# An attention block on one core: two key tiles for each column-tiled visit of TensorE, row maxima of two heads at once with the mask added on VectorE, fp32r masks, and the division by the row sums moved to the output stage

## The chip, the core and the metric

One core of one Trainium2 chip runs the whole program. The metric is the device time of one execution in microseconds. Engines: PE is TensorE (PEld its weight loads), DVE VectorE, ACT ScalarE, POOL GpSimd, SP SyncE, which here only issues DMAs.

## The reference, cut to what matters

Two batches of 2048 rows of 1024 channels, 32 query heads of 32 channels, 8 key and value heads, causal attention, and a gate with a low-rank routed part:

```python
xn = _layernorm(x, axis=-1)
q = (xn @ wq).reshape(b, s, 32, 32); k, v = 8 heads each, repeated 4 times
scores = jnp.where(causal, jnp.einsum('bihd,bjhd->bhij', q, k) * SCALE, finfo.min)
attn = jax.nn.softmax(scores, axis=-1)
s = jnp.einsum('bhij,bjhd->bihd', attn, v).reshape(b, s, 1024) @ wo
g = _silu(xn @ W_base.T + b_base + routed_low_rank(xn))
out = x + s * g
```

## The kernel before

Four functions follow each other, each a block that ends with all engines done: `project` (layer norm, q, k, v, written to scratch in HBM), `attend`, `gate` and `output`. High and low parts (`_hi`, `_lo`) carry fp32 products in fp32r matmuls.

`attend` works on 16 groups (batch and key head), each with 4 query heads (`NREP`). The queries of a group are cut into 4 chunks of 512 (`CPB`, `CH`); chunk c sees 4(c+1) key tiles of 128, so a group has 16, 32, 48 and 64 score tiles, 160 in all. `stage(c)` writes out the order of the operations of chunk c, and every engine walks that one list:

- "T", j, h (L796 to L809): scores of key tile j against the 512 queries of head h, keys on the partitions, into one of two PSUM banks `cols_ps` (`NCOLS`). On the diagonal a second matmul adds the mask (L807, bf16), and the width shrinks to 384, 256, 128. ACT takes the exponential into `probs[j % 4]` (L887). T number h+2 may start only when the exponential of number h is done.
- "S" (L743): scores with the queries on the partitions, only for the row maximum. It runs 72 pieces (`LEAD`) ahead, in one of four banks `rows_ps`; a piece on the diagonal has a mask matmul too (L750, bf16). DVE reduces each piece to a maximum (L905). The maxima of a chunk are turned ("M", L753, L915) and sent by a DMA to the last row of `q_st[c]`, so that T subtracts them.
- "V", j (L810): the weighted values of key tile j, four matmuls for four heads side by side on 32 columns of the array each (`tile_position`), and the same again for the second pass of fp32. "L", j (L826): the row sums of tile j with a matrix of ones, in the same form, but only for the tiles that POOL doesn't add up (`ADDS`); "Y" (L835): the row sums of what POOL has added. V for tile j stands at step j + 2 after the second T, L for it after the fourth. I call one such stay in the column form a visit. V and L of a tile are two visits.
- "O" (ACT copies `o_ps` and `l_ps`), "I" (eight reciprocals of 64 columns on DVE, L949), "N" (DVE multiplies, L956, and SP stores the normalised chunk).

SP walks the same list: it loads the q chunks for the next group, the row of maxima, and stores. In `gate` and `output` TensorE works on one tile of 128 rows after the other, three matmuls for each product, two PSUM banks. In `output` SP's order for tile n is: store half 0, store half 1 (both wait for DVE), then load the attention result, x and g of tile n + 2 (`load`, L1126). ACT rounds to `t_hi`, DVE subtracts to `t_lo`, and DVE's list for tile n is `finish(n)`, then `low(n + 2)`.

Of the kernel before, what the change touches and what calls it, by code (L numbers as in the profile page):

```python
# [483 lines left out]
def pieces_of(c):  # L484

    return [(i, h, p, min(CH, (TPC * c + i + 1) * P - CH * p))
            for i in range(TPC) for h in range(NREP) for p in range(c + 1)]

PIECES = [(c, n == len(pieces_of(c)) - 1, piece) for c in range(CPB) for n, piece in enumerate(pieces_of(c))]
NPG = len(PIECES)
# [3 lines left out]
assert NPG == NTG  # L496
LEAD = 72
TURN_AFTER = 2
NROWS, NCOLS = 4, 2
NSLICE = 8  # L500


def piece_at(i):

    return (i // NPG, *PIECES[i % NPG])


def stage(c):

    steps, old = TPC * (c + 1), TPC * ((c - 1) % CPB + 1)
    order = []
    for j in range(steps):
        for h in range(NREP):
            t = T_OFF[c] + NREP * j + h  # L520
            order.append(("T", j, h))
            order.append(("S", *piece_at(t + LEAD)))
            turned = piece_at(t + LEAD - TURN_AFTER)
            if turned[2]:
                order.append(("M", turned[0], turned[1]))
            if j == 0 and h == 1:
                order += [("V", old - 2, "before"), ("L", old - 2, "before")]
            if j == 0 and h == 3:
                order += [("V", old - 1, "before"), ("L", old - 1, "before"), ("Y", "before")]
            if j == 1 and h == 1:  # L530
                order.append(("O",))

            slot = (NREP * (j - 2) + h) // (1 if c == 0 else 2)
            if 0 <= slot < NSLICE and (c == 0 or h % 2):
                order.append(("I", slot))
            if j >= 2 and h == 1:
                order.append(("V", j - 2))
            if j >= 2 and h == 3:
                order.append(("L", j - 2))
        if j == (3 if c == 0 else 5):  # L540
            order.append(("N",))
    return order
# [5 lines left out]
def before(op):  # L548
    return op[0] in ("O", "I", "N") or op[-1] == "before"


def first_uses():

    out = []
    for i in range(LEAD):
        out.append(("S", *piece_at(i)))
        if i >= TURN_AFTER and piece_at(i - TURN_AFTER)[2]:
            out.append(("M", *piece_at(i - TURN_AFTER)[:2]))
# [4 lines left out]
USES = [sum(op[0] in "SM" for op in st) for st in STAGES]  # L563
NSG = sum(USES)
S_OFF = [len(FIRST_USES) + sum(USES[:c]) for c in range(CPB)]
assert NSG % NROWS == 0


ADDS = {"pool": [[], [0, 1, 3, 4, 6], [0, 1, 3, 4, 6, 7, 9, 10], [0, 1, 3, 4, 6, 7, 9, 10, 12, 13]]}


def adds_through(who, c, j):

    return sum(max(0, len(a) - 1) for a in ADDS[who][:c]) + sum(1 for t in ADDS[who][c][1:] if t <= j)


def adds_of_group(who):
    return adds_through(who, CPB - 1, NJG)


def attend(nc, sc, ident, ident_b, mask_ij, mask_ji, wb, lb, gw_hi, gw_lo):

    ctx = ExitStack()
    with ctx:
# [11 lines left out]
        probs = [sb(f"probs{i}", [P, NREP, CH]) for i in range(4)]  # L596
        added = {who: sb(f"added_{who}", [P, NREP, CH]) for who in ADDS}
        neg_max = [sb(f"neg_max{i}", [P, NREP * TPC, CPB]) for i in range(2)]
        shift = sb("shift", [P, 16], FP32R)
        row = [sb(f"row{i}", [16, P]) for i in range(2)]  # L600
        o_raw = [sb(f"a_o_raw{i}", [P, CH]) for i in range(2)]
        l_raw = [sb(f"l_raw{i}", [P, CH]) for i in range(2)]
        o_sb = [sb(f"o_sb{i}", [P, CH]) for i in range(2)]
        gw_raw = sb("gw_raw", [P, 4, D])
# [669 lines left out]
```

## Time and profile before

| | us |
|---|---|
| median of 3 runs (3853.81 to 3854.62) | 3854.03 |
| span of the profiled execution | 3855.3 |
| PE busy in it | 3712.1 (96%) |
| PEld, DVE busy | 2272.1 (59%), 2212.6 (57%) |
| ACT, POOL busy | 1557.0 (40%), 1379.6 (36%) |

The page gives no other time of the profiled execution than its span; it is 1.3 us over the median. `project` runs to about 670 us, the first exponential of `attend` stands at 703.96 and the last matmul at about 3078, `gate` runs to about 3494, `output` to the end. In the listed rows a busy time counts the overlap of pipelined matmuls once, and a duration is from issue to end, so start-to-start distances tell TensorE's pace, not durations.

### The profile page before, as it was taken

How to read it: one execution, taken by the hardware profiler on the slowest of the kernel's cores; microseconds unless marked ns; L12 is line 12 of the kernel's file. 1: busy time of each engine (PE TensorE's matmuls, PEld its weight loads, DVE VectorE, ACT ScalarE, POOL GpSimd, SP SyncE). 2: the span in 40 equal slices, each digit the busy share in tenths (PEclk: the TensorE clock that was granted, in tenths of full speed). 3: DMA queues.
4: the chain of work that ended last, by engine and by line, in shares of the span. 5: the costliest groups of instructions: out<-in, count | busy, mean ns of one | idle time of the engine just before them, and what ended most of it. 6: DMA issues, size and time to landing. Idle time of an engine off the chain costs nothing. (4 is left out here: it accounts for less than half of the span.)

```text
span 3855.3 us, 66009 instructions
## 1 busy us (share of the span) xinstructions
PE 3712.1 (96%) x21376; PEld 2272.1 (59%) x21376; DVE 2212.6 (57%) x4099; ACT 1557.0 (40%) x3042; POOL 1379.6 (36%) x349
## 2 busy tenths in 40 slices
PE   7999998999999999999999999999999889998999
PEld 6888886544444444444444444444444378887887
DVE  5343332877777777777777677777777322222333
ACT  3122210455555555555555555555555511011000
POOL 0000000465565574565465565555655600000000
PEclk9999998799999999999999999999999999999999
DMA  6555444211101102101101111111010054444555
GB/s 219 167 175 159 153 145 146 79 34 35 46 20 49 38 23 48 39 26 45 43 26 45 37 32 42 35 35 45 21 47 18 6 179 145 137 137 162 191 189 174
DMA packets 232906, 326.87 MB, mean 85 GB/s; under 512 B 16800, under 2 KB 132512, under 8 KB 231072
## 3 DMA queue, kind: packets, MB, share of 16 engines
q1 hardware_dynamic: 229008, 310.48, 26.7%
q10 hardware_dynamic: 3600, 12.58, 1.0%
q8 instruction: 167, 2.74, 0.3%
q14 instruction: 131, 1.07, 0.1%
HBM read 188.25 MB, written 134.22 MB: 84 GB/s over the span
## 5 line engine op out<-in xcount | busy, mean ns | idle before, releaser
L905 DVE TENSOR_REDUCE neg_max<-rows_ps 128x1 f32<-128x512 f32 (+3 forms) x2560 | 1434.3, 602 | 600.7 <-PE rows_ps L747 427.2
L887 ACT ACTIVATE probs<-cols_ps 128x512 f32<-128x512 f32 (+3 forms) x2560 | 1270.4, 533 | 1059.4 <-PE cols_ps L804 542.9
L737 POOL TENSOR_TENSOR added_pool<-added_pool,probs 128x2048 f32<-128x2048 f32 (+2 forms) x272 | 1137.0, 4180 | 296.6 <-ACT probs L887 285.5
L804 PE MATMUL cols_ps<-q_st,k_st 97*128 97x512 f32 (+3 forms) x2560 | 1089.6, 428 | 61.7 <-ACT probs L887 42.9
L747 PE MATMUL rows_ps<-k_st,q_st 96*128 96x512 f32 (+3 forms) x2560 | 1021.7, 405 | 16.9 <-DMA q_st<-scratch_q_hi 16.9
L804 PEld LDWEIGHTS cols_ps<-q_st,k_st 97*128 97x128 f32 x2560 | 488.2, 191 | 820.6 <-ACT probs L887 702.8
L821 PE MATMUL o_ps<-probs,v_st 128*32 128x512 f32 (+3 forms) x5120 | 605.7, 545 | 0.0
L747 PEld LDWEIGHTS rows_ps<-k_st,q_st 96*128 96x128 f32 x2560 | 510.6, 200 | 40.9 <-issue 17.1
L737 POOL TENSOR_TENSOR added_pool<-probs 128x2048 f32<-128x2048 f32 x48 | 219.5, 4573 | 726.3 <-ACT probs L887 726.3
L949 DVE RECIPROCAL l_raw<-l_raw 128x64 f32<-128x64 f32 x512 | 275.3, 540 | 56.2 <-ACT a_o_raw L897 56.2
L438 PE MATMUL acc<-xt_hi,w_hi 128*128 128x512 f32 x704 | 281.6, 400 | 0.6 <-DVE logits L381 0.6
L440 PE MATMUL acc<-xt_hi,w_lo 128*128 128x512 f32 x704 | 277.6, 394 | 0.0
L439 PE MATMUL acc<-xt_lo,w_hi 128*128 128x512 f32 x704 | 276.8, 393 | 0.0
L720 POOL TENSOR_TENSOR gw_lo<-gw_raw,gw_hi 128x1024 fp32r<-128x1024 f32 x9 | 21.0, 2372 | 672.3 <-ACT gw_hi L862 672.3
L750 PE MATMUL rows_ps<-mask_ij,ident_b 128*128 128x128 bf16 x1024 | 241.8, 236 | 0.0
L395 DVE SCALAR_TENSOR_TENSOR out_lo<-acc,out_hi 128x512 fp32r<-128x512 f32 x80 | 55.3, 692 | 324.4 <-ACT out_hi L290 324.4
L1082 PE MATMUL g_acc<-gw_hi,g_t_hi 128*128 128x512 f32 x576 | 225.2, 391 | 16.9 <-DMA g_t_lo<-scratch_hw_lo 16.9
L807 PE MATMUL cols_ps<-mask_ji,ident_b 128*128 128x128 bf16 x1024 | 237.9, 232 | 0.0
L831 PE MATMUL l_ps<-probs,ones 128*32 128x512 f32 (+3 forms) x2176 | 228.0, 491 | 0.0
L1083 PE MATMUL g_acc<-gw_lo,g_t_hi 128*128 128x512 f32 x576 | 224.9, 390 | 0.0
L1084 PE MATMUL g_acc<-gw_hi,g_t_lo 128*128 128x512 f32 x576 | 224.8, 390 | 0.0
L1202 PE MATMUL o_acc<-ow_hi,o_t_hi 128*128 128x512 f32 x512 | 200.4, 391 | 11.2 <-DVE o_t_lo L1168 11.2
(101 smaller groups left out, 3155.0 us busy)
## 6 DMA issues: line engine op xcount, KB each, us to landing
q_st<-scratch_q_hi SPq DMA_DIRECT2D x128, 256.0 KB, 4.4
x_sb<-in_x SPq DMA_DIRECT2D x32, 512.0 KB, 4.0
scratch_xt_hi<-xt_hi SPq DMA_DIRECT2D x32, 512.0 KB, 6.0
scratch_xt_lo<-xt_lo SPq DMA_DIRECT2D x32, 512.0 KB, 6.8
scratch_q_hi<-out_hi SPq DMA_DIRECT2D x64, 256.0 KB, 2.4
scratch_q_lo<-out_lo SPq DMA_DIRECT2D x64, 256.0 KB, 2.9
q_st<-scratch_q_lo SPq DMA_DIRECT2D x64, 256.0 KB, 4.6
scratch_o<-o_sb SPq DMA_DIRECT2D x64, 256.0 KB, 2.4
```

The source lines that it names most:

```text
L438: nc.tensor.matmul(out, lh, rh, start=(k == 0), stop=False)
L439: nc.tensor.matmul(out, lh, rl, start=False, stop=False)
L440: ins = nc.tensor.matmul(out, ll, rh, start=False, stop=(k == KT - 1))
L737: nc.gpsimd.tensor_tensor(added["pool"][:, :, q0:CH], a[:, :, q0:CH], probs[j % 4][:, :, q0:CH], ALU.add).then_inc(pool_added, 1)
L747: ins = nc.tensor.matmul(out[:, 0:keys], q_st[c][0:K1, h, i * P:(i + 1) * P], k_st[kbuf][0:K1, CH * p:CH * p + keys], start=True, stop=p < c)
L750: ins = nc.tensor.matmul(out[:, keys - P:keys], ident_b[:, :], mask_ij[:, :], start=False, stop=True)
L804: ins = nc.tensor.matmul(cols_ps[h % NCOLS][:, q0:CH], k_st[u][:, j * P:(j + 1) * P], q_st[c][:, h, q0:CH], start=True, stop=not diagonal)
L807: ins = nc.tensor.matmul(cols_ps[h % NCOLS][:, q0:q0 + P], ident_b[:, :], mask_ji[:, :], start=False, stop=True)
L821: ins = nc.tensor.matmul(o_ps[h * HD:(h + 1) * HD, q0:CH], v_st[vbuf][:, j, :], probs[j % 4][:, h, q0:CH], start=(j == 0), stop=(j == step ...
L887: nc.scalar.activation(probs[j % 4][:, h, q0:CH], cols_ps[h % NCOLS][:, q0:CH], ACT.Exp) \
L905: nc.vector.tensor_reduce(neg_max[chunk % 2][:, r, p:p + 1], rows_ps[bank % NROWS][:, 0:keys], AX.X, ALU.max, negate=True).then_inc(rows_f ...
L949: ins = nc.vector.reciprocal(l_raw[cp % 2][:, part], l_raw[cp % 2][:, part])
```

## The change

- S: the list is now made of units, two heads of one block of 128 queries and one chunk of keys. Both heads' matmuls go into one slot of two banks (`rows_ps` is 2 slots of 2 banks), and one semaphore count covers both. Below the diagonal DVE reduces both at once; on it there is no mask matmul, DVE runs a tensor_tensor_reduce for each head, which adds `tri` (fp32 in SBUF), writes the sum in bf16 and keeps the maximum. `LEAD` is 40 units, that is 80 pieces.
- T: its mask and the identity are fp32r, no longer bf16.
- V, L and Y become "W": at every even step j it takes the values of tiles j - 4 and j - 3, then the row sums of those of the two that POOL doesn't add, then, at the end of a chunk, those that POOL has added. `probs` has 5 buffers, not 4. POOL's lists are shorter (18 additions for a group, were 20), each addition is cut in two halves of two heads, and it alternates between two sums.
- ACT copies `o_ps` and `l_ps` to buffers that SP stores as they are. The reciprocals and the product leave `attend`. `gate` loads all row sums, inverts them in 8 parts of 128 columns on DVE, and ACT's queue stores them.
- `output` loads for each tile, beside the attention result, the inverted sums with four DMAs (each repeats the 8 rows of a head on 32 partitions), DVE multiplies (`norm`), and SP's and DVE's orders change as shown.
- The loads of `gw_raw` at the start of `attend` have 2 buffers, not 4.

```diff
 def stage(c):
             t = T_OFF[c] + NREP * j + h
             order.append(("T", j, h))
-            order.append(("S", *piece_at(t + LEAD)))
+            ahead, chunk, last, unit = unit_at(t // 2 + LEAD)
+            order.append(("S", ahead, h % 2, chunk, last, unit))
...
+            if j % 2 == 0 and h == 1:
+                order.append(("W", old - 4 + j, "before") if j < 4 else ("W", j - 4))
+            if j == 2 and h == 1:
+                order.append(("K",))
+            if j == 2 and h == 3:
                 order.append(("O",))
...
-ADDS = {"pool": [[], [0, 1, 3, 4, 6], [0, 1, 3, 4, 6, 7, 9, 10], [0, 1, 3, 4, 6, 7, 9, 10, 12, 13]]}
+ADDS = [[], [0, 1, 3, 4, 6], [0, 1, 3, 4, 6, 8, 10], [0, 1, 3, 4, 6, 8, 9, 11, 13]]
...
+            def row_scores(use, slot, kbuf, half, c, i, p, hp):
+                if half == 0:
+                    pe.wait_ge(rows_free, use + 1)
+                keys = keys_of(c, i, p)
+                ins = nc.tensor.matmul(rows_ps[slot][:, half, 0:keys], q_st[c][0:K1, 2 * hp + half, i * P:(i + 1) * P],
+                                       k_st[kbuf][0:K1, CH * p:CH * p + keys], start=True, stop=True)
+                if half == 1:
+                    ins.then_inc(rows_full, 1)
...
+            def unit_max(full, slot, c, i, p, hp):
+                wait_apart(dve, rows_full, full, passed_rows)
+                if p < c:
+                    nc.vector.tensor_reduce(row_max[c % 2][:, 2 * hp:2 * hp + 2, i, p], rows_ps[slot][:, :, :], AX.X, ALU.max) \
+                        .then_inc(rows_free, 1)
+                    return
+                keys = keys_of(c, i, p)
+                for half in range(2):
+                    ins = nc.vector.tensor_tensor_reduce(masked_rows[slot][:, half, 0:keys], rows_ps[slot][:, half, 0:keys],
+                                                         tri[:, CH - keys:CH], 1.0, MASKED, ALU.add, ALU.max,
+                                                         row_max[c % 2][:, 2 * hp + half, i, p:p + 1])
+                ins.then_inc(rows_free, 1)
...
+            def weigh(n, u, c, op):
+                pe.wait_ge(probs_ready, n.lin(NTG, T_OFF[cc] + NREP * (j0 + 2) + NCOLS - back * NTG))
+                for j in (j0, j0 + 1):
+                    ...
+                        ins = nc.tensor.matmul(o_ps[h * HD:(h + 1) * HD, q0:CH], v_st[vbuf][:, j, :],
+                                               probs_of(cc, j)[:, h, q0:CH], start=(j == 0), stop=(j == steps - 1),
+                                               tile_position=(0, h * HD))
...
@@ output, SP
                 for u in range(2):
                     n = Step(pair, u)
+                    if not last:
+                        wait_apart(sp, t_lo_ready, n.lin(1, 1), passed)
+                        load_o(n.lin(1, 2), b, u)
                     for half in range(2):
                         wait_apart(sp, y_ready, n.lin(2, half + 1), passed)
...
                     if not last:
-                        load(n.lin(1, 2), b, u)
+                        load_xg(n.lin(1, 2), u)
@@ output, DVE
+            def norm(n, u):
+                dve.wait_ge(t_loaded[u], n.pair * 80 + 80)
+                nc.vector.tensor_mul(o_raw[u][:, :, :], o_raw[u][:, :, :], l_inv[u][:, :, :]).then_inc(norm_ready, 1)
...
+            norm(Step(0, 0), 0)
+            norm(Step(0, 1), 1)
             low(Step(0, 0), 0)
             low(Step(0, 1), 1)
             with dve.Fori(0, NPAIR - 1) as pair:
                 for u in range(2):
+                    norm(Step(pair + 1, u), u)
                     finish(Step(pair, u), u)
                     low(Step(pair + 1, u), u)
```

## Rows read from the trace of the kernel before

**Rows 1.** Windows of one group and of output: us, then busy by engine

```profile
1746.06:1893.10 147.04, 143.99 (x934) 69.45 (x932) 109.81 (x205) 82.60 (x169) 84.77 (x20) 1.00 0.15 37
3550.00:3855.00 305.00, 301.26 (x1330) 249.12 (x1328) 108.14 (x139) 28.64 (x27) 0.00 (x0) 1.00 0.55 187
```

**Rows 2.** Timeline of PE, one step below the diagonal: start, us, line

```profile
1844.24 0.50 PE L804 MATMUL cols_ps<-q_st,k_st 97*128 97x512 f32 x1
...
1844.82 0.40 PE L804 MATMUL cols_ps<-q_st,k_st 97*128 97x512 f32 x1
...
1845.43 0.50 PE L804 MATMUL cols_ps<-q_st,k_st 97*128 97x512 f32 x1
...
1846.00 0.41 PE L804 MATMUL cols_ps<-q_st,k_st 97*128 97x512 f32 x1
...
1846.48 1.07 PE L821 MATMUL o_ps<-probs,v_st 128*32 128x512 f32 x8
1847.48 0.50 PE L804 MATMUL cols_ps<-q_st,k_st 97*128 97x512 f32 x1
```

**Rows 3.** Timeline of weight loads in that step, with the idle time before

```profile
1845.43 0.19 PEld L804 LDWEIGHTS cols_ps<-q_st,k_st 97*128 97x128 f32 x1 [0.22 <-ACT probs L887]
```

**Rows 4.** Timeline of ACT in that step

```profile
1844.78 1.09 ACT L887 ACTIVATE probs<-cols_ps 128x512 f32<-128x512 f32 x2 [0.93 <-PE cols_ps L804]
1846.05 1.09 ACT L887 ACTIVATE probs<-cols_ps 128x512 f32<-128x512 f32 x2 [0.18 <-PE cols_ps L804]
```

**Rows 5.** Timeline of PE on the diagonal

```profile
1889.24 0.28 PE L804 MATMUL cols_ps<-q_st,k_st 97*128 97x256 f32 x1
...
1889.73 0.22 PE L804 MATMUL cols_ps<-q_st,k_st 97*128 97x128 f32 x1
...
1890.68 0.85 PE L821 MATMUL o_ps<-probs,v_st 128*32 128x384 f32 x8
1891.47 0.33 PE L804 MATMUL cols_ps<-q_st,k_st 97*128 97x128 f32 x1
```

**Rows 6.** Groups by form, 725 to 3130 us: busy, mean ns, idle

```profile
L905 DVE TENSOR_REDUCE neg_max<-rows_ps 128x1 f32<-128x512 f32 x1738 | 1128.6, 681 | 471.5 <-PE rows_ps L747 420.6 <-PE rows_ps L750 34.8 <-issue 5.4
...
L807 PEld LDWEIGHTS cols_ps<-mask_ji,ident_b 128*128 128x128 bf16 x1008 | 98.0, 97 | 105.8 <-issue 70.0
```

**Rows 7.** DVE's product of two SBUF tiles: ns min/median/max

```profile
L956 DVE TENSOR_TENSOR o_sb<-a_o_raw,l_raw x64: 691/1369/2641, 745.4 to 3082.6; 128x512 f32<-128x512 f32 x64
```

**Rows 8.** Timelines around the start and the end of attend

```profile
L720 POOL TENSOR_TENSOR gw_lo<-gw_raw,gw_hi x9: 2352/2377/2382, 675.8 to 694.4; 128x1024 fp32r<-128x1024 f32 x9
...
3079.17 3.43 DVE L949 RECIPROCAL l_raw<-l_raw 128x64 f32<-128x64 f32 x8 [45.62 <-ACT a_o_raw L897]
```

**Rows 9.** Timeline of SP's queue in output, one tile

```profile
3712.10 0.41 SPq L1127 DMA_DIRECT2D o_raw<-scratch_o  x1
...
3713.35 0.38 SPq L1129 DMA_DIRECT2D o_g<-scratch_g  x1
```

**Rows 10.** Timeline of DVE in output, one tile

```profile
3709.86 0.69 DVE L1177 SCALAR_TENSOR_TENSOR o_prod<-o_acc,o_g 128x512 f32<-128x512 f32 x1 [0.69 <-PE o_acc L1204]
3710.59 0.69 DVE L1181 TENSOR_TENSOR o_y<-o_prod,o_x 128x512 f32<-128x512 f32 x1
3717.36 1.23 DVE L1168 TENSOR_TENSOR o_t_lo<-o_raw,o_t_hi 128x1024 fp32r<-128x1024 f32 x1 [6.08 <-ACT o_t_hi L1155]
3718.50 0.68 DVE L1177 SCALAR_TENSOR_TENSOR o_prod<-o_acc,o_g 128x512 f32<-128x512 f32 x1
...
3720.74 0.69 DVE L1177 SCALAR_TENSOR_TENSOR o_prod<-o_acc,o_g 128x512 f32<-128x512 f32 x1 [0.83 <-PE o_acc L1204]
```

**Rows 11.** DMA issues by line: KB each, median us to landing

```profile
v_st<-scratch_v SPq DMA_DIRECT2D x16, 256.0 KB, 7.5
...
out<-o_y SPq DMA_DIRECT2D x28, 256.0 KB, 2.0
```

**Rows 12.** Windows of 1 us in output; last columns DMA share, GB/s

```profile
3717.00:3718.00 1.00, 1.00 (x6) 0.84 (x5) 0.64 (x1) 0.33 (x1) 0.00 (x0) 1.00 0.99 406
```

More of the change, by code:

```diff
@@ L555, in first_uses, with adds_through, attend @@
     for i in range(LEAD):
-        out.append(("S", *piece_at(i)))
-        if i >= TURN_AFTER and piece_at(i - TURN_AFTER)[2]:
-            out.append(("M", *piece_at(i - TURN_AFTER)[:2]))
+        for half in range(2):
+            ahead, chunk, last, unit = unit_at(i)
+            out.append(("S", ahead, half, chunk, last, unit))
+        if i >= TURN_AFTER and unit_at(i - TURN_AFTER)[2]:
+            out.append(("M", *unit_at(i - TURN_AFTER)[:2]))
     return out
 FIRST_USES = first_uses()
-USES = [sum(op[0] in "SM" for op in st) for st in STAGES]
+NFIRST = sum(map(ends_use, FIRST_USES))
+USES = [sum(map(ends_use, st)) for st in STAGES]
 NSG = sum(USES)
-S_OFF = [len(FIRST_USES) + sum(USES[:c]) for c in range(CPB)]
-assert NSG % NROWS == 0
-ADDS = {"pool": [[], [0, 1, 3, 4, 6], [0, 1, 3, 4, 6, 7, 9, 10], [0, 1, 3, 4, 6, 7, 9, 10, 12, 13]]}
[L572 to L581, printed above, removed]
+S_OFF = [NFIRST + sum(USES[:c]) for c in range(CPB)]
+assert NSG % NSLOT == 0
+ADDS = [[], [0, 1, 3, 4, 6], [0, 1, 3, 4, 6, 8, 10], [0, 1, 3, 4, 6, 8, 9, 11, 13]]
+NADD = sum(len(a) - 1 for a in ADDS if a)
+def adds_through(c, j):
+    return 2 * (sum(max(0, len(a) - 1) for a in ADDS[:c]) + sum(1 for t in ADDS[c][1:] if t <= j))
+def attend(nc, sc, ident, ident_r, mask_ji, tri, wb, lb, gw_hi, gw_lo):
     ctx = ExitStack()
@@ L775, in run @@
                     kind = op[0]
-                    if kind in "VLY":
-                        old = op[-1] == "before"
-                        cc = (c - 1) % CPB if old else c
-                        back = 1 if old and c == 0 else 0
-                        steps = TPC * (cc + 1)
-                        to_sum = [j for j in range(steps) if not any(j in ADDS[who][cc] for who in ADDS)]
-                        adders = [who for who in ADDS if ADDS[who][cc]]
                     if kind == "S":
-                        ahead, chunk, _, piece = op[1:]
-                        if piece == pieces_of(chunk)[0]:
+                        ahead, half, chunk, _, unit = op[1:]
+                        if half == 0 and unit == units_of(chunk)[0]:
                             pe.wait_ge(q_loaded[chunk], n.lin(48, 48 * (1 + ahead)))
@@ L845, in _ @@
+                    elif kind == "W":
+                        weigh(n, u, c, op)
+                    use += ends_use(op)
             over_stages(pe, run)
@@ L887, in run @@
-                        nc.scalar.activation(probs[j % 4][:, h, q0:CH], cols_ps[h % NCOLS][:, q0:CH], ACT.Exp) \
+                            g = J_OFF[c] + j - NPROBS
+                            act.wait_ge(values_done, n.lin(NVG, g // 2 + 1 + 3))
+                            back = 1 if g < 0 else 0
+                            c5 = CPB - 1 if back else max(cc for cc in range(CPB) if J_OFF[cc] <= g)
+                            j5 = g + back * NJG - J_OFF[c5]
+                            first_group = isinstance(n.pair, int) and n.pair == 0 and u == 0
@@ L1139, in pair_of_tiles @@
                     if not last:
-                        load(n.lin(1, 2), b, u)
-            load(0, 0, 0)
-            load(1, 0, 1)
+                        load_xg(n.lin(1, 2), u)
+            for u in range(2):
+                load_o(u, 0, u)
+                load_xg(u, u)
             with sp.Fori(0, NPAIR // 2 - 1) as pair:
```

403 lines of the change are left out of this document (201 added, 202 removed).

## The prediction

> **What bounds the kernel now.** I read the windows first. In one whole group of attend (147.04 us, one of 16) TensorE is busy for 143.99 us, DVE for 109.81, ACT for 82.60, POOL for 84.77; in output TensorE is busy for 301.26 of 305 us [rows 1]. So TensorE looks like the bound in both, at full granted clock (1.00, the 2.4 GHz level). But a busy TensorE isn't one at its peak, so the timeline of one step comes second [rows 2]. The reader is to see three distances there, from one T to the next. Just after a visit a pair T, S takes 0.58 us (1844.24 to 1844.82). The third T comes 0.61 us after the second, and its weight load had idled for ACT [rows 3]. From the visit's start to the next T it is 1.00 us (1846.48 to 1847.48). ACT's own timeline tells why the third T waits [rows 4]: the exponential of the first begins at 1844.78, 0.04 us after the T ends (1844.24 + 0.50), takes 0.60, and the T that needs its bank starts 0.05 later, at 1845.43. With two banks that is a loop: two Ts take 0.50 + 0.04 + 0.60 + 0.05 = 1.19 us, however fast TensorE is. After the first head of a tile, where ACT also waits for other engines, the lag is 0.12 instead of 0.04 (1845.93 to 1846.05), and the loop 1.27. So below the diagonal attend is bound by this loop between visits and by TensorE in visits. ACT stands idle in a visit (0.93 us before 1844.78) and can't catch up later, for only two scores lie ready.
>
> **The change part by part.** All sums are against the span, 3855.3 us; the median of the runs is 1.3 lower, and so is my number.
>
> *Price of a pass.* A visit on 512 columns takes 1.00 us, one on 384 columns 0.79 [rows 2, 5]; 128 columns cost 0.21, so 512 cost 0.86 and the switch itself 0.14. The T after it has its weight load exposed, and so has a T that waited for ACT: 0.10 more, for a pair takes 0.58 there, and 0.49 on the diagonal where the weights were loaded in time (1889.24 to 1889.73 [rows 5], T of 256 columns, mask, S of 512). That row also gives the price of a mask: six steps of 128 columns at 0.06 are 0.36, so 0.13 is left for it.
>
> *Merged visits.* By the code a group has 51 visits now (40 V, 11 separate L) and 20 after. If TensorE were the bound, 31 x 0.24 x 16 = 119 us would go. I go through eight Ts between two visits below the diagonal instead. Starts: 0, 0.58, 1.19 (loop), 1.77 (its weights exposed again), 2.45 (loop 1.27), 3.02, 3.64, 4.21; then S and into the visit, 4.78, less 0.06 since three S pieces in ten are narrower, and 0.14 for the switch: 4.86 us besides the passes. Twelve such stretches in a group: 58.3. On the diagonal TensorE sets the pace, with 0.61, 0.55, 0.49, 0.43 for T, mask, S at 512 to 128 columns of T (0.49 is the row): the stretch over widths 512, 384, 256 comes to 4.7, that over 256, 128 and the next chunk's 512 to 4.0. Four of each: 34.8. Passes after, in full widths: V 34, L 14.25, Y 3, so 51.25 x 0.86 = 44.1; before it was 49.5, so the shorter lists of POOL cost 1.5 us a group. ACT's two copies hold the loop up by 0.8 us a chunk, 3.2, as now; the turned shift 0.4 a chunk, 1.6. Sum 142.0, against 147.04.
>
> *Row maxima.* The S masks (1024 of them) vanish from TensorE; in the stretches above they are already left out. On DVE one reduction of 1024 columns stands for two of 512 at 0.68 each [rows 6]: between 0.68 and 1.36, and I take 1.22, near the upper end, since the elements are as many. The two slots free up in larger lumps: unit 3 must wait for the reduction of unit 1. Below the diagonal that comes just in time (unit 1 complete at 1.21, reduced at 2.47, unit 3's first S at 2.79). On the narrow tiles units come every 1.0 us, and I count 0.25 us a chunk for DVE: 1.0 a group. The masked reduction has no row. Its nearest are the plain one (0.68) and the product of two SBUF tiles, 0.69 at least, median 1.37 beside POOL's additions [rows 7]; I take 0.7, since only one of its inputs is in SBUF. The group is then 143.0: 4.0 less, and over 15 full groups -60 us.
> The Trainium skill says the same of it: "SBUF — State Buffer", section "SBUF: two separate sides", has GpSimd and VectorE lock each other out only for a two-port mode or two SBUF inputs. By that the 1.37 doesn't apply; the slow case is a rival below, since no run here shows it.
>
> *fp32r masks in T.* A bf16 identity loads in 0.10 us, an fp32r weight in 0.19 [rows 3, 6]. Either the load hides under the T (and a change of type between two loads vanishes), or it shows on narrow Ts. 1024 x (-0.07 to +0.09) = -70 to +95 us; I take 0, because the T before it is 512 columns wide or has an exposed load in most places.
> The skill's "TensorE: Matmul & The Clock Gate", section "Weight-path perf modes — Fast Weight Load (FWL) and DoubleRow", allows the fast load only for types that aren't fp32. It speaks against this edit: the row agrees for the load (0.10 against 0.19), and the whole price would be the +95 end.
>
> *Start and end of attend.* With two buffers the nine pieces of the gate's weights (POOL 2.38 us each, the last from 694.4 [rows 8]) end later than the first S units do: 0 to +12, taken +4, with the longer lead. At the end the reciprocals (3.43 us [rows 8]) and the product go, but two more tiles of values stand after the last exponential: -3. In gate the reciprocals (8 x about 1 us) lie under the matmuls of a half tile, which take at least the 5.4 us of one in output (half of 10.88 [rows 10]); nothing, and 1 us each if that cover were gone.
>
> *Output.* Here a loop through the DMAs becomes long. SP issues the loads of tile n + 2 after the stores of tile n - 1 and the loads of x and g for n + 1, and DVE must multiply tile n + 2 before it finishes tile n; TensorE waits for that finish to get its bank for n + 1. Count from Y, the end of DVE's work on tile n - 1 (3710.59 + 0.69 = 3711.28 [rows 10]). The first load is issued at Y + 0.82, the next ones 0.6 apart [rows 9]; seven now, so the last at Y + 4.6. The engines then move x, g, the result and the sums, 2 MB, at 406 GB/s at best with a DMA share of 0.99 [rows 12], and about 300 for packets of 512 B; flow starts 1.9 after the issue, so the sums have landed at Y + 2.7 + 2.7 + 1.7 + 1.7 = Y + 8.8. From there norm 1.15 (1.23 long, next start 1.14 later [rows 10]), then four steps of 0.72: the next Y is at 8.8 + 4.0 = 12.8. A tile now takes 10.88 (3709.86 to 3720.74 [rows 10]). So TensorE idles 2.0 us a tile, 29 tiles: +58. At the start norm of both tiles stands ahead of the first low part, behind all fourteen DMAs: +6. Together +64. Bounds: if the last DMA needed only 2.0 us from its issue, it lands at 6.6 and no time is lost; if it needed 7.5, as the loads of values do [rows 11], a tile takes 16.1 and it is +157.
>
> Sum: 3855.3 - 60 + 0 + 1 + 64 = 3860, as a median 3859.
>
> **The rivals.**
> 1. *The sums land in time.* The loss in output begins only when they land later than about Y + 7.6 (norm 1.15 and prod 0.69 must end before tile n + 1 starts at Y + 9.4). If the queue drains 1.2 us sooner than I count, output keeps its pace: 3859 - 58 = 3801. For it: the four DMAs are only 128 KB each, and DMA share is 0.55 on average [rows 1]. Against it: seven issues in a row, and DVE's order.
> 2. *TensorE, not the exponential's loop, is the bound of attend.* Then the visits give 119, the S masks 1024 x 0.13 = 133, less 24 for passes: -228 instead of -60, 3691. Against it is the idle weight load [rows 3], 0.22 us before each third T.
> The skill's "TensorEngine Tiling (Array Packing)", section "Key Properties", has TensorE drained by each change of tiling mode. The row agrees with 0.14 us; by that rule alone each visit saved would count, which is this rival.
> 3. *Slower: the masked maxima wait for POOL.* If tensor_tensor_reduce with `tri` in SBUF takes 1.37 instead of 0.69 [rows 7], a masked unit takes 2.7 us against 1.2 between units, and the S two units later waits; 32 units x 16 x about 0.5 = +250, 4109. It decides once a masked unit takes over about 1.8 us.
> 4. *Slower: the sums land late*, at 7.5 us from the issue: 3859 + 99 = 3958.
>
> **How the numbers follow.** My forecast (output waits, the loop eats most of attend's gain) gets 0.45, with its own range 3815 to 3905 from DVE's lumps and the masks; rival 1 0.30, rival 2 0.10, rival 3 0.07, rival 4 0.08. The range for 8 in 10 leaves out rivals 2 and 3 and the ends of the others: 3765 to 3960. A measurement here can tell about 0.2%, 8 us, from no change. Forecast: faster 0.15, same 0.08, slower 0.22. Rival 1: 0.26, 0.02, 0.02. Rival 2: faster 0.09, same 0.01. Rivals 3 and 4: slower 0.15. Sum: faster 0.50, same 0.11, slower 0.39.
>
> **What would show it.** In output the distance from tile to tile (12.8 against 10.88), TensorE's idle time before a tile with DVE's prod as releaser, and norm's start released by a DMA. In attend a group of about 143 us, the third T still released by the exponential, visits of 0.14 + 0.86 for each pass. The masked reduction at 0.7 us and a 1024-column one at 1.2. The T, mask, S of 128 and 256 columns stays at 0.43 and 0.49, or is up to 0.09 slower if the fp32r load shows. I am wrong if output keeps its pace, if a group is under 140 us, or if DVE holds up TensorE below the diagonal.

## The result

The changed kernel takes 4198.8 us (median of 4 runs, 4185.1 to 4205.8) against 3854.3 us for the kernel before on the same chip: ratio 1.0887, 95% interval 1.0872 to 1.0902. It is 8.9% slower, where 3859 us were forecast, and outside the range. Its span is 4194.2 us, 338.9 more than 3855.3. Read from the two traces by first and last instruction of each stage:

| stretch | before, us | after, us | difference | forecast |
|---|---|---|---|---|
| up to the first exponential | 704.0 | 715.4 | +11.4 | +4 |
| attend, first to last exponential | 2372.0 | 2459.4 | +87.4 | -60 |
| its end and gate | 413.0 | 410.1 | -2.9 | -3 |
| gate's last matmul to output's first | 11.3 | 32.1 | +20.8 | +6 |
| output, 32 tiles | 351.0 | 573.2 | +222.2 | +58 |

The windows of the kernel after that answer to [rows 1]: the same odd group of attend, the even group ahead of it, and output. The columns are as there: us, busy PE, PEld, DVE, ACT, POOL, then PEclk, DMA share, GB/s.

```profile
1797.68:1948.33 150.65, 142.44 (x886) 74.07 (x886) 88.43 (x185) 83.26 (x168) 79.22 (x36) 0.98 0.14 36
1638.14:1797.68 159.54, 146.35 (x885) 75.18 (x884) 88.10 (x185) 83.12 (x168) 79.17 (x36) 0.95 0.14 35
3620.00:4190.00 570.00, 415.63 (x1530) 328.28 (x1529) 152.45 (x186) 31.72 (x30) 0.00 (x0) 0.86 0.56 139
```

TensorE now idles 8 to 13 us in a group, where before it idled 3 in an odd one; in output it idles for 154 us, and its granted clock is 0.86 there on average. Two things are to be explained: the output stage, and an attend that has less work on TensorE (142.4 us busy against 144.0) and takes longer.

**Output.** First DVE's timeline of one tile in the kernel after (it answers to [rows 10]; the bracket is the idle time before), then SP's queue that feeds it ([rows 9]), then the chain that ended last, in order of time.

```profile
4000.97 0.69 DVE L1206 TENSOR_TENSOR o_y<-o_prod,o_x 128x512 f32<-128x512 f32 x1
...
4016.23 1.23 DVE L1189 TENSOR_TENSOR o_raw<-o_raw,o_l_inv 128x1024 f32<-128x1024 f32 x1 [13.43 <-DMA o_l_inv<-scratch_l_inv]
4017.37 0.68 DVE L1202 SCALAR_TENSOR_TENSOR o_prod<-o_acc,o_g 128x512 f32<-128x512 f32 x1
```

```profile
4000.58 1.70 SPq L1157 DMA_DIRECT2D out<-o_y  x2
4002.46 0.35 SPq L1145 DMA_DIRECT2D o_x<-in_x  x1
4002.91 0.40 SPq L1146 DMA_DIRECT2D o_g<-scratch_g  x1
4003.59 0.38 SPq L1139 DMA_DIRECT2D o_raw<-scratch_o  x1
4004.16 3.63 SPq L1141 DMA_DIRECT2D o_l_inv<-scratch_l_inv  x4
```

```profile
3893.76 9.63 DMA o_l_inv<-scratch_l_inv
...
3912.08 9.81 DMA o_l_inv<-scratch_l_inv
...
3930.31 10.12 DMA o_l_inv<-scratch_l_inv
```

The loop is the one the prediction described: seven issues, a landing, norm, and only then the end of tile n that frees TensorE's bank. Its period is 18.4 us instead of 12.8. DVE waits 13.4 us for the row sums before it can do 4 us of work. The chain shows the last of the four DMAs on its way for 8.5 to 11.2 us in each tile, about 9.8 at the median. Windows of 1 us while only these DMAs are under way:

```profile
4012.00:4013.00 1.00, 0.34 (x2) 0.00 (x0) 0.00 (x0) 0.00 (x0) 0.00 (x0) 1.00 0.75 47
4014.00:4015.00 1.00, 0.00 (x0) 0.00 (x0) 0.00 (x0) 0.00 (x0) 0.00 (x0) 1.00 0.76 70
```

The DMA engines are three quarters busy and move 47 to 70 GB/s, where I had put 300.

**Attend.** A stretch in the middle of an odd group, windows of 1 us, and TensorE's timeline at its end:

```profile
1825.00:1826.00 1.00, 0.51 (x3) 0.25 (x2) 1.00 (x4) 1.00 (x3) 0.99 (x1) 1.00 0.00 0
1826.00:1827.00 1.00, 0.58 (x3) 0.39 (x3) 0.28 (x4) 0.91 (x3) 0.00 (x0) 1.00 0.05 20
1827.00:1828.00 1.00, 0.87 (x4) 0.57 (x5) 0.29 (x1) 1.00 (x2) 0.00 (x0) 1.00 0.66 250
...
1830.00:1831.00 1.00, 1.00 (x8) 0.22 (x4) 0.41 (x1) 0.00 (x0) 1.00 (x2) 0.50 0.00 0
1831.00:1832.00 1.00, 1.00 (x8) 0.00 (x0) 0.00 (x0) 0.00 (x0) 1.00 (x1) 0.50 0.00 0
```

```profile
1826.42 0.49 PE L839 MATMUL cols_ps<-q_st,k_st 97*128 97x512 f32 x1 [0.91 <-ACT probs L889]
...
1828.96 3.53 PE L798 MATMUL o_ps<-probs,v_st 128*32 128x512 f32 x16
1832.42 0.54 PE L839 MATMUL cols_ps<-q_st,k_st 97*128 97x512 f32 x1
```

TensorE waited (busy 0.51 and 0.58 of two windows, here while ACT copied O and L out), and then its granted clock is 0.50, the 1.2 GHz level, and a visit of two tiles takes 3.46 us from its start to the next T; at full clock the same x16 takes 1.85. For a part of it ACT has nothing to do (0.00 of two windows). Over attend the kernel before has 50.6 us at the low level, the kernel after 205.8. 6 of these spells begin in attend before, 38 after; one more is under way as attend starts, and its rest, 13 and 18 us, is in the sums. At half speed the difference is at most (205.8 - 50.6) / 2 = 78 of the 87 us.

Not each wait brings the clock down. From 900 to 3000 us the kernel after has 120 windows of 1 us, not at the low level, in which TensorE is busy for less than 0.6, and 32 falls; each fall stands no more than 2.2 us behind such a stretch, but most of the stretches have no fall behind them.

### The profile page after: what moved, and what is told of

The parts are those of the page before. It is cut to its first block and busy times, and to the rows that moved or that the text cites. A ratio compares the mean times of both kernels' runs of the same rounds, so it can differ in the third digit from the quotient of the medians.

```text
span 4194.2 us, 64097 instructions
## 1 busy us (share of the span) xinstructions
PE 3775.0 (90%) x20608; PEld 2392.3 (57%) x20608; DVE 1906.4 (45%) x3821; ACT 1564.8 (37%) x3042; POOL 1290.6 (31%) x603
## 5 line engine op out<-in xcount | busy, mean ns | idle before, releaser
L906 DVE TENSOR_REDUCE row_max<-rows_ps 128x2 f32<-128x1024 f32 x768 | 933.1, 1225 | 725.1 <-PE rows_ps L755 715.8
L738 POOL TENSOR_TENSOR added<-added,probs 128x1024 f32<-128x1024 f32 (+2 forms) x480 | 1040.6, 2193 | 481.4 <-ACT probs L889 481.4
L911 DVE CUSTOM_DVE_ANT_0 masked_rows<-rows_ps,tri 128x128 bf16<-128x128 f32 (+3 forms) x1024 | 458.6, 487 | 304.5 <-PE rows_ps L755 290.2
L738 POOL TENSOR_TENSOR added<-probs 128x1024 f32<-128x1024 f32 x96 | 226.3, 2379 | 717.6 <-ACT probs L889 717.6
L1230 PE MATMUL o_acc<-ow_hi,o_t_hi 128*128 128x512 f32 x512 | 230.5, 450 | 186.5 <-DVE o_prod L1202 154.4
L798 PEld LDWEIGHTS o_ps<-probs,v_st 128*32 128x32 f32 x5120 | 140.2, 114 | 290.9 <-issue 221.7
L842 PE MATMUL cols_ps<-mask_ji,ident_r 128*128 128x128 f32 x1024 | 245.6, 240 | 0.0
L1230 PEld LDWEIGHTS o_acc<-ow_hi,o_t_hi 128*128 128x128 f32 x512 | 111.7, 218 | 224.0 <-DVE o_prod L1202 167.0
L1176 ACT ACTIVATE o_t_hi<-o_raw 128x1024 fp32r<-128x1024 f32 x32 | 33.8, 1057 | 546.8 <-DVE o_raw L1189 533.4
L1189 DVE TENSOR_TENSOR o_raw<-o_raw,o_l_inv 128x1024 f32<-128x1024 f32 x32 | 39.2, 1225 | 426.1 <-DMA o_l_inv<-scratch_l_inv 426.1
```

Of the source, the lines that this page charges most:

```text
L738: nc.gpsimd.tensor_tensor(into[:, heads, q0:CH], other[:, heads, q0:CH], probs_of(c, j)[:, heads, q0:CH], ALU.add).then_inc(pool_added, 1)
L798: ins = nc.tensor.matmul(o_ps[h * HD:(h + 1) * HD, q0:CH], v_st[vbuf][:, j, :], probs_of(cc, j)[:, h, q0:CH], start=(j == 0), stop=(j == s ...
L842: ins = nc.tensor.matmul(cols_ps[h % NCOLS][:, q0:q0 + P], ident_r[:, :], mask_ji[:, :], start=False, stop=True)
L906: nc.vector.tensor_reduce(row_max[c % 2][:, 2 * hp:2 * hp + 2, i, p], rows_ps[slot][:, :, :], AX.X, ALU.max) \
L911: ins = nc.vector.tensor_tensor_reduce(masked_rows[slot][:, half, 0:keys], rows_ps[slot][:, half, 0:keys], tri[:, CH - keys:CH], 1.0, MASK ...
L1230: nc.tensor.matmul(acc[half][:, :], t_hi[u][:, k, :], w_hi[:, k, cols], start=(k == 0), stop=False)
```

## The experiments

Each was timed beside the kernel before on the same chip; that kernel's median was 3853.1 to 3856.6 us in the three rounds, so a difference between times of two rounds carries some 3 us. "Low" is the time in attend at the 1.2 GHz level, counted as above. What a tile of output takes is the median distance from tile to tile.

### Output: the division taken out

```diff
-                for h in range(NREP):
-                    sp.dma_start(l_inv[u][h * HD:(h + 1) * HD, :, :], sc["l_inv"]...partition_broadcast(HD))
-                nc.vector.tensor_mul(o_raw[u], o_raw[u], l_inv[u]).then_inc(norm_ready, 1)
+                dve.sem_inc(norm_ready, 1)
```

> The changed kernel without the division in output: the four loads of inverted sums for each tile and the multiplication are left out, so the attention result isn't divided. Everything else of the change stays, SP's new order too. Theory (the sums' loads and the order on VectorE make all of output's loss): a tile takes 10.9 us again, output loses about 220 us and its start 10, so 3965 to 3975, and what is left over the kernel before, 110 to 120 us, belongs to attend and its start. Rival (SP's new order costs by itself): above 12 us a tile, over 4000.

3964.2 us, ratio 1.0270 (1.0248 to 1.0293). Output is back at its old pace (352.6 us against 351.0), so the division costs 4198.8 - 3964.2 = 235 us, and everything else in the change 110. The way from gate's last matmul to output's first is 14.9 us, against 32.1 with the division and 11.3 before. Attend is nearly unchanged (2464.9 us, low 218.1 in 44 spells): the two losses are separate.

### Output: DVE's order

```diff
-                    norm(Step(pair + 1, u), u)
                     finish(Step(pair, u), u)
+                    norm(Step(pair + 1, u), u)
                     low(Step(pair + 1, u), u)
```

> The changed kernel with one line moved: in output VectorE finishes tile n before it multiplies tile n + 2. Theory (the order on VectorE puts the landing of the sums on the path of every tile): with the order mended a tile takes as long as the DMA engines need for its 2.5 MB, which in the changed kernel is about 14 us (6 for x, g, the result and the stores, 8 for the sums at 60 GB/s), or the old 10.9 us if the slow loads overlap others; so 4199 becomes 4090 (14 us) to 3975 (10.9 us). Rival (the landing itself is the bound, whatever the order): stays at about 18.5 us a tile, 4199.

4018.8 us, ratio 1.0423 (1.0396 to 1.0450). One line moved gives back 180 us: a tile now takes 12.4 us. The groups of DVE in output, kernel after and then this one (columns: busy, mean ns, idle and its releaser; some tiles at the ends left out):

```profile
L1189 DVE TENSOR_TENSOR o_raw<-o_raw,o_l_inv 128x1024 f32<-128x1024 f32 x30 | 36.8, 1225 | 399.9 <-DMA o_l_inv<-scratch_l_inv 399.9
```

```profile
L1189 DVE TENSOR_TENSOR o_raw<-o_raw,o_l_inv 128x1024 f32<-128x1024 f32 x30 | 36.8, 1225 | 174.1 <-DMA o_l_inv<-scratch_l_inv 174.1
```

The landing is no faster, 8.7 us at the median, and DVE still waits 5.8 us a tile for it, but TensorE works meanwhile.

### Output: what makes the DMA slow

Two edits of the kernel after. In the first the four DMAs keep destination, size and number, and read 32 different rows of O's scratch instead of one row 32 times; in the second the repeated source stays, and eight DMAs write all 128 partitions.

```diff
-  sp.dma_start(l_inv[u][h * HD:(h + 1) * HD, :, :], sc["l_inv"][b, :, h, cols].partition_broadcast(HD))
+  sp.dma_start(l_inv[u][h * HD:(h + 1) * HD, :, :], o_src[h * HD:(h + 1) * HD, b, :, cols])     # first
+  for g in range(NKV):                                                                          # second
+      sp.dma_start(l_inv[u][:, g, :], bcast(sc["l_inv"][b, g, :, cols], 1, HD))
```

> The changed kernel with another source for the four loads of each tile in output: 32 different rows of the attention result instead of one repeated 32 times, the same destination, sizes and packets (the result is then multiplied by itself instead of being divided). Theory (the repeated source makes the loads slow, about 60 GB/s): they go at 250 GB/s and more, a tile takes 12 to 13 us instead of 18.4, 4199 becomes 4010 to 4050. Rival (a destination of 32 partitions uses only some of the 16 DMA engines, whatever the source): within 20 us of 4199.

> The changed kernel with the inverted sums loaded by eight DMAs of 64 KB on all 128 partitions for each tile (one for each key head) instead of four of 128 KB on 32 partitions each; the source is still repeated 32 times. Theory (the repeated source is slow): about as now, 4199 within 40 us, or slower by the four further issues (4 x 0.6 us x 29 = 70 us). Rival (32 partitions are the cause): 12 to 15 us a tile, 4010 to 4100.

First 4093.4 us (ratio 1.0620, 1.0598 to 1.0641), second 4278.3 (1.1099). Both medians are of two runs. With different rows a tile takes 15.0 us, short of the 12 to 13 expected; the DMAs land after 6.4 us instead of 8.3, and in the windows behind the landing of the attention result, where the sums' DMAs are left, the engines move 150 and 157 GB/s instead of 47 to 70:

```profile
4012.00:4013.00 1.00, 1.00 (x6) 0.83 (x5) 0.00 (x0) 0.00 (x0) 0.00 (x0) 1.00 1.22 157
4013.00:4014.00 1.00, 1.00 (x6) 0.84 (x5) 0.00 (x0) 0.00 (x0) 0.00 (x0) 1.00 0.83 150
```

With 128 partitions and a repeated source it is slower still (20.5 us a tile), by 79 us, about what the four further issues were put at. So 32 reads of one row cost some 105 us of the 235, and the narrow destination isn't what costs it. Even with different rows the tile isn't back at 10.9. What is left stands with the four further issues, their packets of 512 B and norm; no run parts these.

### Attend: the S masks, and the type of the T masks

Both start from the kernel before. The first drops the S mask matmul and takes the masked maximum with `tri` on DVE, one head at a time; the second only gives T's mask and identity the type fp32r.

```diff
-                if p == c:
-                    ins = nc.tensor.matmul(out[:, keys - P:keys], ident_b[:, :], mask_ij[:, :], start=False, stop=True)
+                if p == chunk:
+                    nc.vector.tensor_tensor_reduce(masked_rows[...], rows_ps[bank % NROWS][:, 0:keys],
+                                                   tri[:, CH - keys:CH], 1.0, MASKED, ALU.add, ALU.max, row_max[...])
```

> The kernel before with one part of the change alone: the row scores have no mask matmul, VectorE adds the mask on the diagonal with tensor_tensor_reduce, piece by piece, in the same four banks. Theory (below the diagonal the exponential's loop hides a mask matmul, so it counts only just after a visit and on the diagonal): 15 to 40 us faster than before, about 3825. Rival (TensorE is the bound everywhere): 1024 x 0.13 us = 133 us faster, about 3720. Rival (the masked reduction waits for POOL, 1.4 us and more instead of 0.7): slower than before.

> The kernel before with the mask and the identity of the T scores in fp32r instead of bf16, nothing else. Theory: within 10 us of before, since in the changed kernel T, mask, S, T at 512 columns takes 0.58 us against 0.59. Rival (the slower weight load of fp32r shows): up to 95 us slower. Rival (the change of type cost something): up to 70 us faster.

The masks on DVE: 3815.0 us, ratio 0.9890 (0.9874 to 0.9907), 41 us less than before, 0.04 us a mask. That is just over the upper end of the theory; both rivals fell. In attend TensorE is busy for 60 us less (2306.2 to 2246.5), 0.06 us a mask instead of 0.13, and idle for 19 us more. The type: 3854.0 us, ratio 0.9995 (0.9986 to 1.0005), nothing. The groups by form of the masked maxima in the kernel after, among them the read of the accumulator that each brings along:

```profile
L911 DVE CUSTOM_DVE_ANT_0 masked_rows<-rows_ps,tri 128x512 bf16<-128x512 f32 x248 | 159.4, 687 | 3.0 <-PE rows_ps L755 0.9
...
L911 DVE DVE_READ_ACCUMULATOR2_ANT row_max<- 128x1 f32 x980 | 81.0, 83 | 0.8
L911 DVE CUSTOM_DVE_ANT_0 masked_rows<-rows_ps,tri 128x128 bf16<-128x128 f32 x244 | 61.4, 287 | 129.8 <-PE rows_ps L755 129.4
```

687 ns on 512 columns, beside POOL's additions: no trace of 1.37.

### Attend: the turned maxima taken out

```diff
-            if h % 2 and turned[2]:
-                order.append(("M", turned[0], turned[1]))
```

> The changed kernel without the division in output (3964 us), and without the turned maxima in attend too: the 64 transposes, the small copies on VectorE and the row's DMA are left out, and nothing is subtracted from the scores (the exponential's scale is 0.1 so that it stays finite). Theory (with two large slots each turn holds TensorE's row scores up by about 1.1 us until a 1024-column reduction is done, and the granted clock then falls to its 1.2 GHz level for some stretches of 3.4 us): 64 x 1.1 = 70 us and at least half of the 78 us that the clock costs go, so 3810 to 3860. Rival (the turns are harmless, the loss is in the visits): above 3930.

3913.4 us, ratio 1.0155 (1.0138 to 1.0172): 51 us less than with the turn, low 177.3 instead of 218.1. The time lies between theory and rival, so neither holds as it stood. The turn costs 0.8 us for each of 64, what it costs in clock included (at most (218.1 - 177.3) / 2 = 20 us), and twice what I had put, but it isn't the main cause.

### Attend: one key tile per visit

```diff
-            if j % 2 == 0 and h == 1:
+            if h == 1:
                 order.append(("W", old - 4 + j, "before") if j < 4 else ("W", j - 4))
-                for j in (j0, j0 + 1):
+                for j in (j0,):
```

> The changed kernel without the division in output (3964 us), with one key tile for each visit, at every step, instead of two at every second; a tile's values and sums still stand in one visit, the buffers and lists stay. So 40 visits for a group instead of 20. Theory (the exponential's loop hides most of what a merged visit saves): 20 to 50 us slower than 3964. Rival (TensorE is the bound): 20 x 16 x 0.24 = 77 us slower, 4040. Rival (the long visits are themselves the cause of attend's loss, since ACT and VectorE stand idle in them and the two slots can't make up for it): faster than 3964, by up to 90 us.

3809.6 us, ratio 0.9881 (0.9865 to 0.9898). 155 us less than with two tiles per visit, with twice the visits and the same arithmetic. Attend takes 2308.6 us, low 39.9 in 4 spells. My theory and the TensorE-bound rival both fell. The third, faster with short visits, has the direction, but the gain is well over its 90 us, and the next experiment shows that long visits alone aren't the cause. What TensorE waited for from 900 to 3000 us (total, times, longest): the kernel before, the one with two tiles per visit (without division), and this one.

```profile
PE cols_ps L804 <- ACT probs L887: 34.8, 57, 0.8
PE cols_ps L804 <- issue: 12.8, 6, 2.4
```

```profile
PE cols_ps L839 <- ACT probs L889: 50.4, 100, 0.9
PE cols_ps L839 <- issue: 29.8, 6, 5.1
PE rows_ps L755 <- DVE row_max L906: 26.0, 53, 0.6
...
PE rows_ps L755 <- DVE row_max L911: 9.4, 22, 0.6
```

```profile
PE cols_ps L839 <- ACT probs L889: 18.6, 66, 0.5
PE cols_ps L839 <- issue: 13.8, 6, 2.6
...
PE rows_ps L755 <- DVE row_max L906: 1.1, 2, 0.6
```

Of attend's 156 us (2464.9 to 2308.6), (218.1 - 39.9) / 2 = 89 at most are granted clock, and TensorE idles 94 us less (161.3 to 67.3); against both stands the work of twice the visits. The "issue" waits stand at the loop's back edge, once in two groups: 5.0 us each against 2.3, some 20 us over the kernel. The rest of the idle time is above all waits for exponentials and for slots. The trace has the branch back itself; the kernel before and the one with two tiles per visit (ns, min/median/max; the shortest is the last pass, which leaves the loop):

```profile
L641 PEldq COMPARE_BRANCH  x7: 83/3842/4062, 1014.3 to 2801.2; - x7
```

```profile
L633 PEldq COMPARE_BRANCH  x7: 76/5520/5742, 1034.4 to 2892.9; - x7
```

TensorE's queue needs 3.8 us for it before and 5.5 with two tiles per visit, where the other engines need under 0.1. Matmuls already queued cover the first 1.9 us of it before, and only 0.8 here. Single visits have 3.8 and 1.8. Why the branch itself takes longer isn't shown.

### Attend: two key tiles per visit, in the kernel before

```diff
-            if j >= 2 and h == 1:
-                order.append(("V", j - 2))
-            if j >= 2 and h == 3:
-                order.append(("L", j - 2))
+            if j >= 3 and j % 2 and h == 1:
+                order += [("V", j - 3), ("L", j - 3), ("V", j - 2), ("L", j - 2)]
```

> The kernel before with nothing changed but its visits: V and L of two key tiles in one visit at each odd step (20 visits in a group instead of 51). Theory (visits of two tiles are what costs attend its time): slower than before, 3900 to 4000, with more than 30 spells of low clock. Rival 1 (only fewer mode switches count): 31 x 16 x 0.14 to 0.24 us = 69 to 119 us faster, 3735 to 3785. Rival 2 (the loss in the changed kernel needs its two slots of 1024 columns beside the long visits; with four slots of 512 the visit is covered): 3840 to 3870.

3861.2 us, ratio 1.0008 (0.9998 to 1.0019): rival 2, and both my theory and the gain by mode switches fell. Beside four slots of 512 columns the long visits leave the time as it is. But they aren't covered: from 900 to 3000 us S now waits 26.8 us for row maxima, against 26.0 and 9.4 in the kernel with large slots and none in the kernel before.

```profile
PE rows_ps L744 <- DVE neg_max L902: 26.8, 42, 0.9
```

In attend TensorE is busy for 43 us less (2306.2 to 2263.3) and idle for 47 us more (65.8 to 112.9): what 31 visits fewer in a group save, 0.09 us each with the longer time at the low level in it, is lost in waits. The lengths of attend side by side, with low time:

| | short visits | visits of two tiles |
|---|---|---|
| four slots of 512 columns | before: 2372.0 (50.6) | 2376.2 (71.1) |
| two slots of 1024 columns | single visits: 2308.6 (39.9) | without division: 2464.9 (218.1) |

So 156 us are lost where the visits of two tiles stand in the changed kernel, and 4 us where they stand in the kernel before. Which other part of the change they need isn't shown: the rows of the table differ in the slots, and also in the number of probability buffers, in the S masks and in POOL's lists and halves. No run has the changed kernel with four small slots. The clock differs too, and not by the number of waits alone: of the windows counted above the kernel before with two-tile visits has 98, the kernel after 120, but 10 falls against 32.

### Attend: V and L joined, in the kernel before with masks on DVE

```diff
-                order.append(("V", j - 2))
-            if j >= 2 and h == 3:
-                order.append(("L", j - 2))
+                order += [("V", j - 2), ("L", j - 2)]
```

> The kernel before with the S masks on VectorE (as in the first experiment) and, besides, L of a key tile directly behind V of the same tile, in one column-tiled visit: 11 visits fewer in a group (51 to 40), no other order changed. Theory (short visits are harmless and each one saved gives back its two mode switches): 11 x 16 visits x 0.14 to 0.24 us = 25 to 42 us below the first experiment's 3815, so 3773 to 3790. Rival (a visit of eight passes already holds up T and S, as one of sixteen does in the changed kernel): 3815 or more.

3803.7 us, ratio 0.9862 (0.9844 to 0.9879). That is 1.4% below the kernel before and the fastest of all complete kernels here. It is above the 3773 to 3790 I expected and below the rival's 3815: 11 visits fewer in a group gave 13.5 us of attend (2331.0 to 2317.5), 0.08 us a visit instead of 0.14 to 0.24. TensorE's busy time in attend fell by 23.7 us (2246.5 to 2222.8), 0.13 a visit, and 10 of them came back as idle time.

### Attend: does the granted clock follow the waits?

```diff
+                    if kind == "S" and turn_slot is not None:
+                        for _ in range(4):
+                            nc.tensor.transpose(rows_ps[turn_slot][0:16, 1, 0:P], shift[:, :].bitcast(FP32), ident[:, :])
```

> The changed kernel without its division, with four extra transposes of the maxima (into the unused half of the turn's own slot, read by no one) between the turn and the next S, where TensorE waits 1.1 us for a slot: 256 extra matmuls of 0.21 us, about 55 us of TensorE work that lies in waits. Theory (the granted clock falls because TensorE waits there): of the 44 spells of low clock, the 14 that begin at steps 9 and 10 of the last chunk, behind the turn at step 9, are gone but for 3 at most, the others stay, and the time falls by 10 to 25 us from 3964 although work was added. Rival (the clock falls for another reason, the long visits' form for one): the 14 stay, and the time is 3964 to 3990.

3963.8 us, ratio 1.0257 (1.0234 to 1.0279). The same place of the same group, windows and TensorE's timeline, first without and then with the four extra transposes:

```profile
1926.00:1927.00 1.00, 0.48 (x2) 0.17 (x1) 1.00 (x2) 0.73 (x2) 1.00 (x1) 1.00 0.00 0
1927.00:1928.00 1.00, 0.89 (x3) 0.68 (x4) 0.25 (x2) 0.11 (x1) 1.00 (x2) 0.68 0.00 0
1928.00:1929.00 1.00, 1.00 (x5) 0.78 (x3) 0.28 (x1) 0.60 (x1) 1.00 (x1) 0.50 0.04 8
```

```profile
1925.99 0.49 PE L839 MATMUL cols_ps<-q_st,k_st 97*128 97x512 f32 x1
1927.12 0.60 PE L755 MATMUL rows_ps<-k_st,q_st 96*128 96x512 f32 x1 [0.64 <-DVE row_max L906]
```

```profile
1926.00:1927.00 1.00, 0.88 (x6) 0.43 (x5) 1.00 (x2) 0.72 (x2) 1.00 (x1) 1.00 0.00 0
1927.00:1928.00 1.00, 0.92 (x4) 0.79 (x5) 0.21 (x2) 0.23 (x2) 1.00 (x2) 1.00 0.00 0
1928.00:1929.00 1.00, 0.84 (x6) 0.38 (x4) 0.81 (x1) 0.93 (x2) 1.00 (x1) 1.00 0.04 8
```

```profile
1926.28 0.60 PE L824 MATMUL rows_ps<-ident,shift 128*16 128x128 f32 x4
1927.08 0.50 PE L756 MATMUL rows_ps<-k_st,q_st 96*128 96x512 f32 x1 [0.20 <-DVE row_max L913]
```

The S behind the turn comes at the same time, but TensorE is busy for 0.88 of the window instead of 0.48, and the clock stays at 1.00. None of the 14 spells at steps 9 and 10 of the last chunk is left. So at this place the fall hung on the wait. The other half of the expectation failed: fewer but longer spells stand elsewhere, above all in chunk 1 behind ACT's copies (88.7 us begin in that chunk, where it was 61.4), the low time is as before (219.9 us in 31 spells), and so is the kernel's. Filling one gap of several moved the loss and didn't remove it. Why the others grew is open. The copies are the commoner place anyway: without the extra transposes 26 of the 44 spells begin at step 3 or 4 of a chunk, right behind them.

### The change with both parts mended

The single visits and DVE's later norm together, in the complete changed kernel; the diffs are those above.

> The whole change with two parts of it mended: one key tile per column-tiled visit, V and L of it together (as in the experiment with single visits), and in the output stage DVE's division of tile n+2 behind the end of tile n. Theory (the two costs are independent and add up): 3810 for attend's part + (4019 - 3964) = 55 for the division: 3855 to 3875, about the kernel before. Rival (a fast attend does not bring the output stage's cost along unchanged): outside 3840 to 3890.

3870.7 us, ratio 1.0031 (1.0021 to 1.0042), so still slower than before by 0.3%, clear of the noise. The two costs add up as expected: 328 of the 344 us are back. Attend is 59 us shorter than before (2312.8 against 2372.0), the start is 12 us later, and output with its approach takes 66 us more. The division in the output stage eats what attend gains.

## Why the prediction was wrong

The prediction failed in two steps: the landing of the sums in output, which was put 5.8 us too early in every tile, and the merged visits of attend, priced at full clock and with a slot always free for S.

**Output, the step that was mis-sized most: +58 taken, +222 measured.** The mechanism was right (the loop through SP's seven issues, the landing, norm ahead of finish), and its first half too: the first load is issued at Y + 0.8, and the last of the four DMAs of the sums is on its way at Y + 4.5 (4006.18), as taken. The term that failed is the transfer: "about 300 for packets of 512 B" had no row behind it (the windows of 285 to 360 GB/s behind 3714 us of the kernel before have x, g and the attention result in a mix). The engines move 47 to 70 GB/s, and the sums land at Y + 14.6 (4001.66 to 4016.23) instead of Y + 8.8. With 3.9 for DVE that is 18.4, the period seen. The bound of 7.5 us from the issue was that of another DMA, with large packets and different rows; the measured 9.8 lies outside it. A bound from the nearest row wasn't a bound, because that row didn't have the property that mattered, the repeated source.

**Start of output, +6 taken, +21 measured**: the same term, fourteen DMAs behind one another; without the sums it is +3.6.

**Merged visits, -60 taken for attend, +87 measured: the pass model held, the stretch between visits didn't.** Two passes and a switch, 0.14 + 2 x 0.86 = 1.86 us, are what x16 takes at full clock (by the rows it is 4 x 0.21 = 0.84 for a pass and 0.16 for the switch; x16 against x8 gives 0.85). The sum of 143.0 us for an odd group is what the kernel with single visits takes (142.9), though it was made for double ones, which take 150.2. That agreement is luck. Left out were three things. The granted clock was taken as 1.00 for good, because [rows 1] has it so; that row's TensorE is 98% busy, and the change made it wait. S waits for its slot (35 us in 2100, 2.5 us a group where 1.0 was taken), and behind the turn I put 0.4 us where 0.8 is right. And I scaled up a group without the loop's back edge: every second group holds it, and these take 150.8 us on average before and 158.7 after, the others 147.0 and 150.1. The size of these parts is shown, why the clock falls so much more often in the changed kernel is not.

**The exponential's loop as the bound between visits: right in its main consequence, for other reasons in part.** The TensorE-bound rival wanted 119 us for the visits and 133 for the S masks. Alone, the visits gave 0 and the masks 41. But waits explain only a part of the difference. The prices were too high: TensorE's busy time fell by 43 us for the visits (0.09 a visit, and 0.13 where V and L were joined, not 0.24) and by 60 for the masks (0.06 each, not 0.13). All of the 43 and 19 of the 60 came back as idle time, and of the 47 us that it idles more without the 31 visits, 30 are waits for DVE's row maxima and not for exponentials.

**Row maxima: right in their durations.** 1.225 us for 1024 columns (1.22 taken), 0.69 + 0.08 for a masked one of 512 (0.7 taken), no contention with POOL, so rival 3 is out. "Just in time" for the slots was wrong, as said above. **fp32r masks: right**, 0. **Start of attend**: +11 instead of +4, within its 0 to +12 (POOL's last piece of the gate's weights begins at 704.3 instead of 694.4; two buffers and the longer lead weren't parted); **end of attend and gate**: -2.9 as taken.

**Rivals and chances.** Rival 4 had the right cause (the sums land late) and 0.08 of the chance, at half its size: 99 us over the forecast, where output and its start came to 179. Its own sum was 6 us too high, since the start was in the 157 and in the forecast both. Rival 1, with 0.30, had it backwards. The range ended where the bound of one DMA ended, although nothing in the trace excluded a longer one.

## What to carry to other kernels

A DMA of a form that the trace doesn't hold (here small packets by themselves, from a source row read many times) has no upper bound from its neighbours: give it a wide one, and put nothing that frees another engine behind its landing in an in-order queue. An edit that saves work on a 98% busy TensorE by making its bursts longer and its neighbours' buffers coarser can turn saved work into waits, and the waits can come with a lower granted clock; check each half of such an edit alone, and with the other, for here two-tile visits cost 4 us of attend in the kernel before and 156 in the changed one. And look at TensorE's busy and idle time apart: a time that stays the same can hide a saving and a new wait of one size. The division by row sums cost about 55 us behind its broadcast from HBM even in the better order, and the fastest complete kernel here is one that left it in attend (3803.7 us).

## What the runs showed of the hardware

- A repeated source row: 47 to 70 GB/s at a DMA share of about 0.75, against 150 to 157 for different rows of the same packet size, landing after 8.3 against 6.4 us.
- The granted clock fell to 0.50 in the middle of dense work, behind windows in which TensorE was busy for 0.48 to 0.58; filled with useless transposes, the same place kept 1.00. But the loss reappeared elsewhere, and most windows of this kind bring no fall (120 with 32 falls in the kernel after, 98 with 10 in the kernel before with two-tile visits).
- The wait at a loop's back edge on TensorE ("issue") was 2.1 us in the kernel before and 5.0 in the one with two tiles per visit: the branch took its queue 3.8 and 5.5 us, of which queued matmuls covered 1.9 and 0.8.
- A mask matmul of 128 columns less is 0.06 us of TensorE's busy time here, a column-tiled visit less 0.09 to 0.13.
- tensor_tensor_reduce on PSUM and SBUF runs at the plain reduction's speed, 0.69 us on 512 columns, plus 0.08 for its accumulator.
